# A four-stage transformer block on one core: second A operand made before the first mask, a piece of the key split issued a stage later, the bias addition apart from its load, and the last quad's maxima turned later

## The reference

```python
x = x + attn_a(layernorm(x))      # 16 heads of width 8, full softmax over 1024 keys
x = x + ffn(layernorm(x))         # three layers with +1/-1 weights, 128 -> 512 -> 512 -> 128
x = x + attn_b(layernorm(x))      # 8 heads of width 16: see below
x = x + ffn(layernorm(x))
# attn_b, for each head: q and v are relu projections; a weight per channel ("metric") comes from the batch's mean;
# dist = sqrt(weighted squared distance to each of the last 64 tokens); the 32 nearest are kept,
# exp(-dist), normalised, weighs their v; a gated term is added, the result is times q, then times the decoder
```

## Time and profile before

| | value |
|---|---|
| median of 3 runs | 2963.69 us |
| the profiled execution's own time | 2964.93 us |
| its span | 2963.2 us |
| busy: TensorE, VectorE, ScalarE, GpSimd | 2411.7, 2112.0, 2263.2, 688.7 us |
| granted TensorE clock, mean | 0.921 of full |

### The profile page before, as it was taken

How to read it: one execution, slowest core, us unless ns; L and a number is a source line. 1 busy time by engine, 2 the same in 40 slices (tenths; PEclk the granted TensorE clock), 3 DMA queues, 4 the chain that set the end, 5 groups by cost and what they waited for, 6 DMA issues and landing times.

```text
span 2963.2 us, 60847 instructions
## 1 busy us (share of the span) xinstructions
PE 2411.7 (81%) x21171; PEld 1048.0 (35%) x21171; DVE 2112.0 (71%) x10282; ACT 2263.2 (76%) x3151; POOL 688.7 (23%) x869
## 2 busy tenths in 40 slices
PE   4788778888788887988888897888888888887666
PEld 1112242244332443334432443324433344224444
DVE  5801778957797668966789577876689667982695
ACT  4798668977699677987689776996779877994432
POOL 3020115111251114401152112511134011311331
PEclk6599789999899999999889998999999999999887
DMA  3011001100011001210011000110012000000000
GB/s 87 30 46 43 2 19 48 50 18 6 23 56 43 17 8 28 65 31 9 20 44 54 18 6 23 54 42 17 6 35 65 31 9 12 14 17 1 17 20 11
DMA packets 98518, 84.79 MB, mean 29 GB/s; under 512 B 19954, under 2 KB 79540, under 8 KB 98212
## 3 DMA queue, kind: packets, MB, share of 16 engines
q1 hardware_dynamic: 97968, 80.41, 9.2%
q10 hardware_dynamic: 244, 0.49, 0.1%
HBM read 55.32 MB, written 25.44 MB: 27 GB/s over the span
## 4 chain that ended last, share of the span: by engine, by line
ACT 34%; PE 33%; DVE 19%; issue 6%; POOL 5%; SPq 2%; DMA 0%; ACTq 0%; DVEq 0%; POOLq 0%
PE banks L802 30%; ACT PT L1141 17%; DVE xn L1473 4%; ACT pq L1128 4%; DVE h L1476 3%; DVE pq L1260 2%; ACT xn L1086 2%; ACT hparts L1152 2%; POOL Aop L781 2%; PE banks L809 2%; ACT h L1153 2%; ACT h L1054 1%; DVE h L1458 1%; ACT Bs L1054 1%; POOL qkf L728 1%
## 5 line engine op out<-in xcount | busy, mean ns | idle before, releaser
L1141 ACT ACTIVATE PT<-banks 128x1024 f32<-128x1024 f32 x1024 | 996.6, 1038 | 47.4 <-PE banks L802 44.7
L1260 DVE CUSTOM_DVE_ANT_0 pq<-pq,banks 128x512 f32<-128x512 f32 x1024 | 653.4, 683 | 175.5 <-ACT pq L1128 174.8
L1128 ACT ACTIVATE pq<-banks 128x1024 f32<-128x1024 f32 x512 | 523.2, 1023 | 223.5 <-PE banks L802 198.1
L802 PE MATMUL banks<-PT,Vg 128*9 128x512 f32 x4096 | 545.9, 605 | 2.3 <-ACT PT L1141 2.3
L802 PE MATMUL banks<-Q,K 51*128 51x512 bf16 x2048 | 391.0, 393 | 139.9 <-ACT PT L1141 113.3
L802 PE MATMUL banks<-K,Q 48*128 48x512 bf16 x2048 | 360.9, 431 | 80.6 <-ACT pq L1128 37.2
L762 POOL TENSOR_TENSOR hparts<-h,hparts 128x512 fp32r<-128x512 f32 x112 | 140.5, 1272 | 1009.2 <-ACT h L1153 1009.2
L1473 DVE MATCH_REPLACE8 xn<-h,xn 128x96 f32<-128x96 f32 x1536 | 352.2, 241 | 0.0
L802 PE MATMUL banks<-hparts,W 128*128 128x512 f32 x1024 | 303.9, 426 | 39.6 <-ACT h L1153 27.8
L802 PEld LDWEIGHTS banks<-Q,K 51*128 51x128 bf16 x2048 | 96.2, 93 | 620.4 <-ACT PT L1141 534.9
L1476 DVE MAX8 h<-xn 128x8 f32<-128x96 f32 x1536 | 263.0, 243 | 0.0
(11 more groups left out here) (207 smaller groups left out, 3256.3 us busy)
## 6 DMA issues: line engine op xcount, KB each, us to landing
Vw<-scratch_v SPq DMA_DIRECT2D x256, 51.0 KB, 2.1
scratch_k<-pq SPq DMA_DIRECT2D x24, 384.0 KB, 3.1
K<-scratch_k SPq DMA_DIRECT2D x126, 72.0 KB
qkf<-in_hidden_states SPq DMA_DIRECT2D x16, 512.0 KB, 4.4
scratch_q<-pq SPq DMA_DIRECT2D x24, 256.0 KB, 2.3
Q<-scratch_q SPq DMA_DIRECT2D x126, 48.0 KB
K<-scratch_k SPq DMA_DIRECT2D x126, 48.0 KB
scratch_v<-Bs SPq DMA_DIRECT2D x8, 544.0 KB, 3.5
```

What stands on the lines that cost most here:

```text
L802: return pe.matmul(o, l, r, start=start, stop=stop)
L1128: act.activation(cut(g), ring_pair if work is TURN0 and g % 2 else pair[0], ACT.Relu).then_inc(diff_out.sem, 1)
L1141: act.activation(PT[:, at:at + 2, :], pair[g % ESLOTS], ACT.Exp, scale=1.0 if i % 8 < 4 else -1.0).then_inc(probs.sem, 1)
L1260: dve.tensor_tensor_reduce(r, r, pair[1 + g % 2][:, par, :], 1.0, -3.0e38, ALU.subtract, ALU.max, mred[:, par, i, qt:qt + 1]).then_inc(max ...
```

## The change

It moves stages and computes the same. `aop` of tile 1 goes from the second half's first slot to the last slot of the first half, ahead of `dev` 0, in turns 1 to 7 and in the tail. `leading(b, 1)` goes from `qk` to `split` 0. The bias addition becomes a stage `bias` at 0.8; the load stays at 0.6. The `mturn` of quad 3 goes from 0.02 to 0.1 of the second half, in turns 0 to 7. Turns 2 to 6 get lists numbered one by one with absolute ring uses; the stages in them are the same.

```diff
@@ the slots
-            (1, [("gate", 0)]), (2, [("hebb", 0), ("hebb", 1)]), (2, [("aop", 0)]), (2, [("dist", 0)]), (2, [("dev", 0)])]
+            (1, [("gate", 0)]), (2, [("hebb", 0), ("hebb", 1)]), (2, [("aop", 0)]), (2, [("dist", 0)]), (2, [("aop", 1), ("dev", 0)])]
...
-        (3.0, [(_u >= 2, "decd", _u - 2), (_next, "aop", _u + 1), (_here, "vload", _u), (_here, "top", (_u, 0))]),
+        (3.0, [(_u >= 2, "decd", _u - 2), (_last and _next, "aop", _u + 1), (_here, "vload", _u), (_here, "top", (_u, 0))]),
...
-MTURNS = [...], [(0.02, [("a", "mturn", NQUAD - 1)])]
+MTURNS = [...], [(0.1, [("a", "mturn", NQUAD - 1)])]
...
-    two.append([(0.6, [("a", "residual", 0)])])
+    two.append([(0.6, [("a", "residual", 0)]), (0.8, [("a", "bias", 0)])])
@@ GpSimd
-                    if stage == "residual":
+                    if stage == "bias":
                         pool.wait_ge(*res_in.at(b, 1))
                         pool.tensor_tensor(xres[:, :, :], xres[:, :, :], bob[:, :].unsqueeze(1).broadcast_to([P, NU, P]),
...
-                        for w in range(2):
-                            leading(b, w, work)
+                        leading(b, 0, work)
                     if (stage, n) == ("split", 0):
+                        leading(b, 1, work)
                         leading(b, 2, work)
@@ numbering
-TURN, TURN_USE, _ = numbered(phases(True, True, True), _k1 - NR)
+TURNS = []
+for _c in range(2, NB - 1):
+    _work, _use, _k = numbered(phases(True, True, True), _k)
+    TURNS.append((_work, _use))
...
-                go(TURN, TURN_USE, c, h=c + 1, a=c, o=c - 1, p=c - 1, q=c - 2)
+                go(*TURNS[c - 2], c, h=c + 1, a=c, o=c - 1, p=c - 1, q=c - 2)
```

More of the change, by code:

```diff
@@ L154 @@
 MROWS = [(((n + 1) * QGROUPS - 0.2) / GROUPS, [("a", "mrow", n)]) for n in range(NQUAD)]
-MTURNS = [(((n + 1) * QGROUPS + 2.1) / GROUPS, [("a", "mturn", n)]) for n in range(NQUAD - 1)], [(0.02, [("a", "mturn", NQUAD - 1)])]
+MTURNS = [(((n + 1) * QGROUPS + 2.1) / GROUPS, [("a", "mturn", n)]) for n in range(NQUAD - 1)], [(0.1, [("a", "mturn", NQUAD - 1)])]
 FIRST_V = [(0.0, [("a", "v", 0), ("a", "v", 1)])]
@@ L230 @@
 FIRST, FIRST_USE, _k = numbered(HEAD, 0)
-TURN0, TURN0_USE, _k0 = numbered(phases(True, False, False), _k)
-NR = sum(uses(stage, n) for _, stage, n in phases(True, True, True))
-TURN1, TURN1_USE, _k1 = numbered(phases(True, True, False), _k0 - NR)
-TURN, TURN_USE, _ = numbered(phases(True, True, True), _k1 - NR)
-TURN7, TURN7_USE, _k7 = numbered(phases(False, True, True), _k1 - NR)
-LAST, LAST_USE, _ = numbered(TAIL, _k7)
-assert NR % 2 == 0
+TURN0, TURN0_USE, _k = numbered(phases(True, False, False), _k)
+TURN1, TURN1_USE, _k = numbered(phases(True, True, False), _k)
+TURNS = []
+for _c in range(2, NB - 1):
+    _work, _use, _k = numbered(phases(True, True, True), _k)
+    TURNS.append((_work, _use))
+TURN7, TURN7_USE, _k = numbered(phases(False, True, True), _k)
+LAST, LAST_USE, _ = numbered(TAIL, _k)
 class Count:
@@ L254, with __init__ @@
 class Ring:
-    def __init__(self, banks, sem, name, uses):
+    def __init__(self, banks, sem, name):
         self.banks = banks
-        self.ready = Count(sem(f"{name}_ready"), uses)
-        self.evicted = [Count(sem(f"{name}_evicted{i}"), uses // 2) for i in range(2)]
+        self.ready = Count(sem(f"{name}_ready"), 0)
+        self.evicted = [Count(sem(f"{name}_evicted{i}"), 0) for i in range(2)]
     def bank(self, k):
@@ L305, in hybrid_block_kernel @@
         ring_pair = banks[:, 6:8, :]
-        R = Ring(psum[6:8], sem, "ring", NR)
+        R = Ring(psum[6:8], sem, "ring")
         scratch_q = nc.dram_tensor("scratch_q", [PARTS, P, T], BF16, kind="Internal").ap()
```

## The result

The changed kernel took 2986.3 us (median of 8 runs, 2978.87 to 2994.09), the kernel before in the same comparison 2969.17 us (8 runs, 2961.8 to 2973.69): a ratio of 1.0061, 95% interval 1.0049 to 1.0073. It is slower, by about 18 us (0.0061 of 2969), and outside my range of 2959 to 2977. The median of before was 5.5 us higher in this comparison than in the three runs that I had; 18 us, against my +5.6, is the error to explain.

The account below looks back on a forecast made before the run. No engine was taken to bound the whole (ScalarE busy 76%, VectorE 71%), VectorE where the halves meet. Terms +1.5 - 2.0 + 1.5 - 1.0 + 5.6 = +5.6 us on 2963.69 gave 2969.3 us, range 2959 to 2977.

Parts of the forecast that it names:

- step 4: Last quad's maxima turned later, behind the next batch's transposes: a 0.8 us stall in turns 0 to 6, +5.6 us.
- rival (c): Stall at the later turning falls on TensorE's lower clock, about 1.3 us seven times: 2978.4 us; chance 0.15.
- step 1: A operand 1 ahead of the first mask: +1.5 us over turns 1 to 6, -2.0 turn 7, +1.5 tail.
- Rival (a): Removed TensorE waits where a turn's halves meet count in full, seven times 3.3 us: 2946.7 us; chance 0.05.
- (b): The later turning of the last quad's maxima is free because TensorE catches up: 2963.7 us; chance 0.20.
- (d): Mask ends before VectorE splits the maxima: -1.2 instead of +0.4 us in six turns, 2959.7 us; chance 0.10.
- Steps 2 and 3: Split's second half a stage later: zero; bias addition moved behind mask 7: -1.0 us over six turns.

Follow-up runs that it names:

- the other kernel: The changed kernel with the last quad's maxima turned at 0.1025 instead of 0.1 of the second half; 0.9996 of the kernel before.
- the control: The kernel before, unchanged, run and profiled once more; ratio 0.9999.
- the tail alone: The kernel before with A operand 1 ahead of mask 0 in the tail only; ratio 1.0010, +3 us.
- A operand 1 alone: The kernel before with only A operand 1 ahead of mask 0, in turns 1 to 7 and the tail; ratio 1.0023, +7 us.

## Why the prediction was wrong

The sum without step 4 was +1.5 - 2.0 + 1.5 - 1.0 = 0.0 us, and the kernel whose turning stands one group later measured 0.9996 (0.9979 to 1.0013). So the error is one term. That these others fit is in part luck: the tail cost about 3 us where I had 1.5, turns 1 to 6 about nothing where I had 1.5.

**Step 4 is the step that failed.** I wrote +5.6 us: the stall of 0.8 us, seven times, arriving whole at ScalarE and staying. The stall was there, behind the transposes and before PT, as written: 0.5 to 0.6 us in five turns, 1.1 and 2.0 in the other two. What failed is that I took its length for its cost. Where the clock's course did not change (turns 1 and 4), the delay was caught up with, to 0.0 and 0.2 us. Elsewhere the stall fell where TensorE already ran at 1.2 GHz, lengthened that stretch by 3.4 us in turns 2, 3, 5 and 6 (in turns 2, 3 and 6 with two new ones later in the half) and brought one of 6.8 us in turn 0, where the other kernel has none and the kernel before one of 3.4; these five turns lost 14.6 us, and without the stall the kernel is 17 us faster. This is rival (c), in its mechanism and its place. I gave it 0.15. That its price fits (5.6 + 9.1 = 14.7 us against 14.9) is luck: it has 2.1 us in every turn, and the turns lost from 0.0 to 3.4. The rows spoke for it: the clock of 0.82 said that TensorE ran at 1.2 GHz for part of just this stretch, and my own step 1 had moved TensorE's idle from ahead of product 1 to ScalarE's wait at the norm (2.48 us in turn 3), some 9 us ahead of the turning's new place. The wrong choice was to price a stall of TensorE at a low clock by its length.

Rival (c) with my other terms is 2978.4 us, and 2983.9 with the median of before as it stood in the comparison; the 2.4 us that are left to 2986.3 are less than medians of the kernel before differ by (2963.69 to 2970.81). Rival (a) fell with the norm's wait of 1.90 us, and (b) with the 16 and 17 us that the two kernels without the stall gained, though in turns 1 and 4 TensorE did catch up as it says; of (d), the split ran on behind the mask as the forecast had it, not ahead of it. Its sum was off by 0.9 us: -1.2 in six turns in place of the +1.5 gives 2960.6, not 2959.7, which the result does not hang on.

**Step 1.** In turns 1 to 6 it went nearly as written: the norm's wait was 1.3 to 2.6 us, 1.90 in turn 3 (2 to 3 expected, and it stood in the place of the removed one), the variance came 0.5 us later (+0.4 counted), and the split's first piece was held by the mask. The half microsecond was made up otherwise than I had it, so that it fits is in part luck: the scaling took 1.08 us, not 1.56, and that first piece 1.82 us, not near 1. One reading of mine was off: the wait at the norm stands in three of the six turns of the trace of before (2, 3 and 6), not in four, and in the control's in one. The second halves with the turning out of the way are 169.7 and 169.8 us, as before; my +1.5 us is within what single profiles scatter. That ScalarE gains nothing where it stands at the norm held. With the norm's wait removed as well, the two profiles have 0.7 and 1.2 us a turn less, against a scatter of 0.9 us between profiles of unchanged turns, so a gain there is likely and not shown. One sentence of step 4 was false: the old place of the turning would not have cost nothing, but would have held TensorE 3.74 us for VectorE. Turn 7 gained 2.6 us (157.2 and 157.8 before, 154.9 after) where I had 2.0, but not by step 1 alone as I had it: with the turning at its old place it took 158.0 and 158.9 us. The tail lost 2.4 us at the mask, as calculated; of that I took only 1.5, on the ground that a later wait gives part of it back. Measured are +3 us for the tail alone, and 2.7 and 6.7 us between the medians of the two pairs of kernels that differ in it (2970.25 and 2967.51; 2969.28 and 2962.63). My upper bound of 2.5 was probably too tight; the interval of the tail alone (-1 to +7 us) does not exclude it.

**Steps 2 and 3.** -1.0 was counted for both, -1.5 us measured, with an interval that holds both that and zero. VectorE's operation of up to 2.40 us now lasts at most 1.050 us, not 0.29:

```profile
L1492 DVE TENSOR_TENSOR h<-h,sq x64: 291/292/1050, 483.5 to 2952.1; 128x128 f32<-128x128 f32 x64
```

**What stays open.** Why the clock answers so strongly in turns 2, 3 and 6 and not at all in 1 and 4 is not shown: the clock had another course ahead of these halves, and no run here varied that alone. Nor is it shown why new stretches at 1.2 GHz appear as late as 54 and 142 us into the half. Whether the tail costs 3 or 6 us is not settled either.

## What to carry to other kernels

A stall of TensorE has two prices: its length, which can be caught up with (to 0.0 and 0.2 us here), and what runs slower behind it if the granted clock is already below full there (up to 3.4 us a turn here, for a stall of 0.5). Read the clock of the stretch before pricing the stall; where it is low, the instruction that waits is better put behind a group that is ready. And when a wait is removed from an engine, look at the next instruction that shares a buffer with the work behind the wait: here the turning needed product 1's bank, and at its old place waited 3.74 us for it, where 3.14 had been removed.

The best version here moves A operand 1 in the turns only, puts the turning at 0.045 and the variance ahead of product 1's subtraction (steps 2 and 3 as in the changed kernel): 2962.63 us against 2970.1, ratio 0.9980 (0.9964 to 0.9995), faster than both kernels.

## What the runs showed of the hardware

The same work takes one of a few lengths, by how much of it ran at 1.2 GHz and where. A first half with identical instructions took 173.98 us at 0.97 of full clock and 179.06 at 0.93, in one profile of the changed kernel, and the other kernel repeats both to 0.05 us. In the profiles of all kernels but the one with A operand 1 alone, the first halves of turns 2 to 7 lie between 173.9 and 179.6 us: those with 10 us at 1.2 GHz took 173.9 to 174.1, those with 24 us 178.9 to 179.1, and those with 14 us, but for one, 175.1 to 176.2. With 17 or 20 us the amount alone does not tell: they took 176.6 to 179.6. How much of the spread between timed runs of one kernel comes this way is not shown: over 113 runs of the kernel before (2957.53 to 2984.41 us) time and mean granted clock go together only loosely (correlation -0.5). A term of a few us can't be read from a single profile's length.

A small VectorE instruction can be held for the whole of a GpSimd operation: the first piece of the split, 0.18 us when free, started 0.03 us behind the mask and took 1.82 us, until its end (before at most 1.171 us). The Trainium skill's page "SBUF — State Buffer", section "Who interferes with whom", has it that the one which issues first keeps the shared pair of ports for its whole instruction, and names tensor_scalar among the operations that can take that pair; these rows agree.
